# Seven block products for eight in the gate and up projections, and the down projection's weights kept in scratch memory

## The reference

```
x = layernorm(x + self_attention(x))
x = layernorm(x + cross_attention(x, ctx))
W[k,n] = scales[g_idx[k],n] * (w4[k,n] - (z4[g_idx[k],n] + 1))     # for gate, up, down
h   = silu(x @ Wg) * (x @ Wu)       # [1792,1024] @ [1024,2752], twice
out = layernorm(x + h @ Wd)         # [1792,2752] @ [2752,1024]
```

## Time and profile before

| what | value |
|---|---|
| median of 3 runs | 1928.49 us (1924.17 to 1934.58) |
| profiled execution | 1928.87 us, span 1927.2 us |
| PE busy | 1816.8 us, 94% of the span |
| DVE busy | 855.8 us, 44% |
| ACT busy | 445.2 us, 23% |
| POOL busy | 393.0 us, 20% |
| matmuls of 128x448, f16, in gate, up and elsewhere | 4464, busy 863.4 us |

### The profile page before, as it was taken

How to read it: one execution, slowest core, us unless ns; L and a number is a source line. 1 busy time by engine, 2 the same in 40 slices (tenths; PEclk the granted TensorE clock), 3 DMA queues, 4 the chain that set the end, 5 groups by cost and what they waited for, 6 DMA issues and landing times.

```text
span 1927.2 us, 26598 instructions
## 1 busy us (share of the span) xinstructions
PE 1816.8 (94%) x10192; PEld 1023.6 (53%) x10192; DVE 855.8 (44%) x1333; ACT 445.2 (23%) x676; POOL 393.0 (20%) x277
## 2 busy tenths in 40 slices
PE   5798899897999869999999999999999999999998
PEld 3566644586878734454444445444545444444443
DVE  5688551656788854434443444344343210111111
ACT  3222110444565532222222222222221200000000
POOL 0222377233333321111111111111111100000000
PEclk9899999999999989999999999999999999999999
DMA  9242561699999942122112111211221321221220
GB/s 312 69 147 81 152 197 44 136 200 230 240 235 237 232 97 57 39 45 50 44 35 60 35 44 35 60 41 38 48 44 41 111 90 64 102 102 61 92 102 22
DMA packets 298812, 196.10 MB, mean 102 GB/s; under 512 B 258368, under 2 KB 272768, under 8 KB 296580
## 3 DMA queue, kind: packets, MB, share of 16 engines
q1 hardware_dynamic: 292516, 192.19, 39.4%
q10 hardware_dynamic: 6240, 3.15, 0.6%
HBM read 105.11 MB, written 50.34 MB: 81 GB/s over the span
## 4 chain that ended last, share of the span: by engine, by line
PE 54%; issue 26%; DVE 6%; DMA 6%; SPq 5%; POOL 2%; ACT 1%; POOLq 0%; DVEq 0%; ACTq 0%
PE psum L1306 52%; SPq L1738 4%; DMA arena<-arena 3%; DMA arena<-in_x 1%; DVE arena L725 1%; POOL small L944 1%; PE psum L1517 1%; POOL arena L953 1%; PE psum L1535 1%; DMA x_parts_scratch<-arena 1%; DMA arena<-in_L_xattn_Wq 1%; DVE arena L832 1%; DVE arena L500 1%; DVE logits L686 0%; DVE arena L406 0%
## 5 line engine op out<-in xcount | busy, mean ns | idle before, releaser
L1306 PE MATMUL psum<-arena 128*128 128x448 f16 (+7 forms) x9404 | 1746.9, 347 | 51.8 <-DMA arena<-arena 25.7
L1306 PEld LDWEIGHTS psum<-arena 128*128 128x128 f16 (+3 forms) x9404 | 973.1, 107 | 806.6 <-issue 92.5
L1060 POOL TENSOR_TENSOR arena<-arena 128x1024 f16<-128x1024 f32 (+1 forms) x64 | 136.1, 2126 | 659.0 <-ACT arena L1248 659.0
L886 DVE SCALAR_TENSOR_TENSOR arena<-psum,small,arena 128x448 f32<-128x448 f32 x84 | 57.4, 684 | 412.4 <-PE psum L1306 412.4
L926 DVE SCALAR_TENSOR_TENSOR arena<-psum,small,arena 128x512 f32<-128x512 f32 x28 | 21.0, 751 | 327.4 <-PE psum L1306 327.4
L944 POOL TENSOR_TENSOR small<-small 112x1 f32<-112x1 f32 (+1 forms) x46 | 49.9, 1084 | 507.3 <-DVE small L387 507.3
L1248 ACT ACTIVATE arena<-arena 128x1024 f16<-128x1024 f32 (+1 forms) x65 | 68.7, 1057 | 274.2 <-DVE arena L872 274.2
L1261 ACT ACTIVATE arena<-arena 128x448 f16<-128x448 f32 (+1 forms) x88 | 50.7, 577 | 289.0 <-DVE arena L886 289.0
L1018 POOL TENSOR_TENSOR arena<-arena 128x224 f16<-128x224 f32 x64 | 55.7, 870 | 126.2 <-ACT arena L1161 126.1
L870 DVE TENSOR_TENSOR arena<-arena,psum 128x1024 f32<-128x1024 uint32 x65 | 79.4, 1221 | 2.6
L892 DVE TENSOR_TENSOR arena<-arena 128x448 f16<-128x448 f32 (+1 forms) x88 | 55.0, 625 | 57.1 <-ACT arena L1261 57.1
(11 more groups left out here) (189 smaller groups left out, 756.2 us busy)
## 6 DMA issues: line engine op xcount, KB each, us to landing
h_scratch<-arena SPq DMA_DIRECT2D x84, 224.0 KB, 2.7
arena<-h_scratch SPq DMA_DIRECT2D x13, 1376.0 KB, 6.0
arena<-in_ctx SPq DMA_DIRECT2D x32, 512.0 KB, 5.4
arena<-in_x SPq DMA_DIRECT2D x32, 448.0 KB, 5.6
x_scratch<-arena SPq DMA_DIRECT2D x32, 448.0 KB, 3.6
arena<-in_L_ffn_down_qweight SPq DMA_DIRECT2D x21, 512.0 KB
x_parts_scratch<-arena SPq DMA_DIRECT2D x16, 448.0 KB, 5.5
arena<-in_ctx SPq DMA_DIRECT2D x16, 448.0 KB
```

The lines of the kernel that those rows point to most:

```text
L886: dve.scalar_tensor_tensor(h_f[0:n, :], up[0:n, :], sc_u[0:n, :], g_act[0:n, :], ALU.mult, ALU.mult).then_inc(s_hf, 1)
L1060: pool.tensor_tensor(dst[1], src, dst[0], ALU.subtract).then_inc(s_wl, 1)
L1306: mm = pe.matmul(out, a, r, start=(k == 0), stop=(k == len(pairs) - 1))
```

## The change

From chunk 4 to chunk 20 (17 chunks) gate and up are computed together with Strassen's scheme. The 1792 rows are cut in two halves and the inner dimension of 1024 in two halves; the two columns of the block product are gate and up. Eight block products of 12 matmuls (4 inner blocks by 3 passes) become seven, once for each `b` of two (448 rows of each half). The seven use four row operands that are sums (T1 to T4, made once, kept in `xsum`) and four weight operands that are sums (S1, S2, S3, S4, made for each chunk by `weight_sums`: four DVE operations of 512), besides plain blocks. Seven DVE additions of 448 and one ACT copy for each `b` put the results together (`six`, `quarters_second`, `gate_first`, `up_first`, `first_copied`).

The row sums are made during chunks 0 to 3, which keep the old products. A *pair* p is batch p and batch p + 8. For each of the 8 pairs SP loads both from `x2_d` into `xab` (`load_pair`), POOL makes the sums in place (`row_sums`), ACT writes two high parts (`sum_hi`), DVE two low parts (`sum_lo`), and SP transposes both into `xsum` (`load_sums`). There is one buffer `xab`: the next pair is loaded once both low parts of the last are made. Two pairs are handled in each of the chunks 0 to 3. In every list below, `chunk` is the function of an unchanged chunk (0 to 3, and 21).

```
+            def row_sums(p):            # POOL
...
+                pool.wait_ge(s_tx, TX0 + 32 * (p + 1))
+                pool.tensor_tensor(two2, two2, two1, ALU.subtract).then_inc(s_tb, 1)
+                pool.tensor_tensor(two1, two1, one1, ALU.subtract).then_inc(s_tb, 1)
+                pool.wait_ge(s_tb, TB0 + 4 * p + 2)
+                pool.tensor_tensor(one1, two2, one1, ALU.add).then_inc(s_tb, 1)
+                pool.wait_ge(s_tb, TB0 + 4 * p + 3)
+                pool.tensor_tensor(one2, one2, one1, ALU.subtract).then_inc(s_tb, 1)
...
             def chunk(i, s, more):
                 if more:
-                    for m in range(1 if known(i, NI) and i == NI - 2 else 2):
-                        low_part(3 * i + 2 + m, [wgu[1 - s][m][:, l, :, :] for l in range(2)], m)
+                    low_part(3 * i + 2, 1 - s, 0)
+                    row_sums(2 * i)
+                    low_part(3 * i + 3, 1 - s, 1, mixed(i + 1))
+                    row_sums(2 * i + 1)
...
+            def sum_hi(p, i):
+                act.wait_ge(s_tb, TB0 + 4 * p + 4 - 2 * i)
+                if p:
+                    act.wait_ge(s_tt[i], TT0 + 16 * p)
+                act.activation(xabp[i][0:S, 0, :].rearrange("p (c q) -> p c q", c=KC),
+                               xab[i][0:S, :].rearrange("p (q c) -> p c q", c=KC), ACT.Identity,
+                               scale=XF).then_inc(s_th, 1)
...
             def chunk(i, s, e, more):
+                q = 3 * i + 2
                 hidden(i, 0)
                 if more:
-                    dequant(3 * i + 2, 0, 1 - s, e + s)
+                    dequant(q, 0, 1 - s, e + s)
+                    sum_lo(2 * i, 1)
                 hidden(i, 1)
-                if more and not (known(i, NI) and i == NI - 2):
-                    dequant(3 * i + 3, 1, 1 - s, e + s)
+                if more:
+                    masked(q + 1, 1, 1 - s, e + s)
+                    scaled(q + 1, 1, s_cmb if mixed(i + 1) else None)
+                    if mixed(i + 1):
+                        weight_sums(q + 1, i + 1)
+                    sum_lo(2 * i, 0)
                 if is_last(i):
                     dequant(down_no(i), 2, s, i)
                 hidden(i, 2)
                 if not is_last(i):
                     dequant(down_no(i), 2, s, i)
+                    sum_lo(2 * i + 1, 1)
                 hidden(i, 3)
+                if not is_last(i):
+                    sum_lo(2 * i + 1, 0)
...
+            def load_pair(p):
+                if p:
+                    sp.wait_ge(s_tl, TL0 + 2 * p)
+                for i in range(2):
+                    sp.dma_start(xab[i][0:S, :], rows(x2_d, p + i * NB // 2)).then_inc(s_tx, 16)
+            def load_sums(p, i):
+                sp.wait_ge(s_tl, TL0 + 2 * p + 2 - i)
+                sp.dma_start_transpose(xsum[i].rearrange("p l k t -> p (l k) t")[:, :, p * S:(p + 1) * S],
+                                       xabp[i][0:S, :, :].rearrange("p l d -> p (l d)")).then_inc(s_tt[i], 16)
```

SP in `chunk`:

```
+                parts = NGATHER - 1 if is_last(i) else 3 * i + 2
+                sp.wait_ge(s_wf, parts)
+                sp.wait_ge(s_wh, parts)
+                sp.wait_ge(s_wl, parts)
+                if 1 <= i < NI - 1:
+                    store_wd(i - 1, 1 - s)
                 load_down(i, w_down)
                 if w_next:
                     load_chunk(i + 2, s, w_next)
-                if isinstance(i, int) and i == NI - 1:
+                if i < NP:
+                    load_pair(2 * i)
+                    for k in (1, 0):
+                        load_sums(2 * i, k)
+                    load_pair(2 * i + 1)
+                if is_last(i):
+                    sp.wait_ge(s_pr, PR0 + 14 * (NI - 1 - NP))
                     load_first_tile()
+                    for k in range(2):
+                        sp.wait_ge(s_wds[k], WS0 + 16 * (NI // 2 - 1))
+                    for k in range(3):
+                        load_wd(k)
                 for u in range(2):
                     sp.wait_ge(s_hh, 4 * i + 2 * u + 3)
                     sp.wait_ge(s_hl, 4 * i + 2 * u + 3)
-                    half = slice(u * TT // 2, (u + 1) * TT // 2)
-                    for l in range(2):
...
+                if i < NP:
+                    for k in (1, 0):
+                        load_sums(2 * i + 1, k)
```

PE in the 17 changed chunks, and its wait ahead of them:

```
+            def mixed_chunk(i, s, e):
+                last = known(i, NI)
+                for b in range(2):
+                    v = 2 * (i - NP) + b
+                    bank = mixed_banks(s, b)
+                    if b == 0:
+                        pe.wait_ge(s_wl, 3 * i)
+                    pe.wait_ge(s_ad, AD0 + 7 * v - 5)
+                    seventh(bank[0], s, "G1", "X11", b)
+                    if b == 0:
+                        if last:
+                            gather_last(3 * i + 2, 1 - s, e + s)
+                        else:
+                            gather_gu(3 * i + 2, 0, 1 - s, e + s)
+                        pe.wait_ge(s_wl, 3 * i + 1)
+                    pe.wait_ge(s_ad, AD0 + 7 * v - 2)
+                    seventh(bank[1], s, "S2", "T2", b)
+                    if b == 1:
+                        gather_down(down_no(i), i)
+                    pe.wait_ge(s_ad, AD0 + 7 * v - 1)
+                    seventh(bank[2], s, "S1", "T1", b)
+                    pe.wait_ge(s_ad, AD0 + 7 * v)
+                    seventh(bank[3], s, "S3", "T3", b)
+                    if b == 0 and not last:
+                        gather_gu(3 * i + 3, 1, 1 - s, e + s)
+                    pe.wait_ge(s_cp, CP0 + v + 1)
+                    seventh(bank[0], s, "S4", "X22", b)
+                    pe.wait_ge(s_ad, AD0 + 7 * v + 1)
+                    seventh(bank[1], s, "G2", "X21", b)
+                    pe.wait_ge(s_ad, AD0 + 7 * v + 4)
+                    seventh(bank[2], s, "U2", "T4", b)
...
+            with pe.Fori(NP // 2, NI // 2 - 1) as e:
                 for s in range(2):
-                    chunk(2 * e + s, s, e, True)
-            chunk(NI - 2, 0, NI // 2 - 1, True)
+                    mixed_chunk(2 * e + s, s, e)
+            mixed_chunk(NI - 2, 0, NI // 2 - 1)
```

DVE there:

```
+            def mixed_chunk(i, s, e):
+                q = 3 * i + 2
+                last = known(i, NI)
+                v = 2 * (i - NP)
+                bank = mixed_banks(s, 0)
+                dequant(q, 0, 1 - s, e + s)
+                six(v, 0, bank)
+                if not last:
+                    masked(q + 1, 1, 1 - s, e + s)
+                quarters_second(v, 0, bank)
+                if not last:
+                    scaled(q + 1, 1, s_cmb)
+                gate_first(v, 0, bank)
+                summed(v, 4)
+                hidden_f32(i, 0, g_d, g_c)
+                up_first(v, 0, bank)
+                hidden_lo(i, 0)
+                summed(v, 7)
+                hidden_f32(i, 1, g_b, g_a[0])
+                if not last:
+                    weight_sums(q + 1, i + 1)
+                hidden_lo(i, 1)
+                v, bank = v + 1, mixed_banks(s, 1)
+                six(v, 1, bank)
+                dequant(down_no(i), 2, s, i)
+                quarters_second(v, 1, bank)
+                gate_first(v, 1, bank)
+                summed(v, 4)
+                hidden_f32(i, 2, g_d, g_c)
+                hidden_lo(i, 2)
+                up_first(v, 1, bank)
+                summed(v, 7)
+                hidden_f32(i, 3, g_b, g_a[1])
```

More of the change, by code:

```diff
@@ L1263, in chunk, with high_sums @@
+            def high_sums(q, s):
+                act.wait_ge(s_wf, q + 1)
+                high_of_operands(s, 4, OPS)
+                high_of_operands(s, 2, 4).then_inc(s_wh, 1)
             def chunk(i, s, more):
+                q = 3 * i + 2
                 hidden(i, 0)
                 if more:
-                    high_part(3 * i + 2, wgu[1 - s][0][:, 0, :, :], 0)
+                    high_part(q, 1 - s, 0)
+                    sum_hi(2 * i, 1)
                 hidden(i, 1)
-                if more and not (known(i, NI) and i == NI - 2):
-                    high_part(3 * i + 3, wgu[1 - s][1][:, 0, :, :], 1)
+                if more:
+                    if mixed(i + 1):
+                        high_sums(q + 1, 1 - s)
+                    else:
+                        high_part(q + 1, 1 - s, 1)
+                    sum_hi(2 * i, 0)
@@ L1277, in _ @@
             for m in range(2):
-                high_part(m, wgu[0][m][:, 0, :, :], m)
+                high_part(m, 0, m)
             x2_hi(NB - 1, 1)
-            with act.Fori(0, NI // 2 - 1) as e:
+            for i in range(NP):
+                chunk(i, i % 2, True)
+            with act.Fori(NP // 2, NI // 2 - 1) as e:
                 for s in range(2):
-                    chunk(2 * e + s, s, True)
-            chunk(NI - 2, 0, True)
+                    mixed_chunk(2 * e + s, s, e)
+            mixed_chunk(NI - 2, 0, NI // 2 - 1)
@@ new lines, in seventh, with mixed_chunk @@
+            def seventh(out, s, weights, rows_, b):
```

(17 more changed lines are left out.)

394 lines of the change are left out of this document (291 added, 103 removed).

## The result

The changed kernel takes 1960.39 us (median of 4 runs, 1958.92 to 1965.4) against 1928.2 (1924.17 to 1934.58): ratio 1.0172, 95% interval 1.0148 to 1.0196. It is slower by a little under 2%, and inside the range, 15 us above the forecast. Its profiled execution spans 1958.2 us, 31.0 more than before.

The account below looks back on a forecast made before the run. Gate and up were taken to be bound by PE. From 1928.9 us, 65 lost in chunks 0 to 3, 63 saved in the 17 chunks and 14 lost at the end gave 1945 us, range 1898 to 1985.

Parts of the forecast that it names:

- The 17 chunks: Chunks 4 to 20, seven products for eight: 34.1 us per chunk for 37.84, 63 us saved, bounds 78 and 41.
- The wait at the gather of down: Chunks 4 to 20: PE's gather of down waits for DVE's last weight sum, 0.55 us in each chunk.
- my walk: One seven-product chunk stepped through from PE's first product at 0: last weight sum ends at 22.0, PE reaches down's gather at 21.45.
- the six more ends: Chunks 4 to 20: 14 shorter products for 8 add six product ends, 0 to 0.9 us per chunk, taken as 0.3.
- The upper bound of 35.4: Chunks 4 to 20: longest time per chunk in us, with the wait twice as long and ends at 0.15.
- Chunks 0 to 3: Row pairs form a serial chain that PE waits for: 48.7 us per chunk, loss 65 us in all, bounds 51 and 95.
- The stride: Chunks 0 to 3, reads at 32 bytes: sum_hi 2.09 us, sum_lo taken as 1.7, range 1.22 to 2.1.
- The end: End of gate and up: PE begins tile 0 at about +36 us after chunk 20, not +23; cost 14, upper bound 20.
- the small store's place in the queue: End of gate and up: the store of chunk 21's h stands behind 8.7 MB of loads, delaying PE's start; cost 13 us.
- My other case: End of gate and up: the queue lets the small store pass, PE starts at +23 and waits for groups; cost 6 us.
- B: Rival, chunks 0 to 3: the pairs hide and only the last transpose, about 5 us, is seen; 1885 us, chance 0.17.
- C: Rival, chunks 4 to 20: DVE, held by POOL, becomes the bound; 36.2 us per chunk, 1981 us in all, chance 0.18.

Follow-up runs that it names:

- The short low part: In chunks 0 to 3 POOL's low part of the down weights cut to 8 of 1024 columns, against the changed kernel: chunks 0 to 3 take 234.4 us for 240.8.
- the kernel with the small piece last: Changed kernel with all loads issued before the small second piece of tile 0's h, awaited by PE just before its use: end stretch 60.6 us for 67.6.
- the last pair early: Against one pair a chunk plus small piece last: pairs loaded and summed earlier, the last behind chunk 7's gate weights; 1886.57 us against 1929.82, ratio 0.9793.

## Why the prediction came out as it did

**The 17 chunks: right, 10 us too cautious.** 34.1 forecast, 33.42 measured. The wait at the gather of down came where I had put it and for the reason given, but with 0.13 us for 0.55. In the trace, from PE's first product of a chunk on, DVE starts the addition behind the seventh product at 16.96 (17.05 in my walk), PE would reach the gather at 21.40 (21.45), and the last weight sum ends at 21.47 (22.0). I had added full durations on DVE (0.69 for each sum), but the starts of these sums lie 0.60 to 0.72 apart. Without the wait PE needs 33.29, and not 33.55: the six more ends, for which I took 0.3 us, cost 0.04. The upper bound of 35.4 should be 35.25 by its own terms. DVE's last weight sum and PE are within 0.1 us of each other here; by this reading a longer chain on DVE at that place would cost at once, which no run shows. The stretch gained 72.6 and not 17 x 4.42 = 75, since chunk 4 began at a lower clock.

**Chunks 0 to 3: right mechanism, mis-sized by 23 us.** The engines that wait, and the places, are those named. In chunk 0 the chain held to its steps up to the second transpose: the pair at 733.4 (735 forecast), the first `sum_lo` 7.0 behind it (6.9), up weights 12.5 (12.65), the second `sum_lo` 17.6 (17.55). Then three terms were short, for 5.9 of the 6.0 us that a chunk took longer:
- From there to the second pair's landing: 8.0 us for 6.6. I counted one load at 0.35; the pair is two, and their issue takes 1.72.
- The third `sum_lo` ended 9.1 behind its pair's landing, not 6.9: it took 4.44. I had POOL's fourth sum ahead of it, not POOL's low part of the down weights, which follows without a gap. The short low part shows that it is this, 1.4 us a round by itself in the mean of three.
- From the last `sum_lo` to the next landing: 14.9 for 12.55, in the second transpose and SP's chunk head.

In chunk 3 the pairs lie 30.9 us apart, for 25.6 in the other chunks: there the weight sums and their high and low parts lie on the path, and I had counted the sums alone, 2.9. Three chunks were 18.5 us longer and chunk 3 was 6.1 longer; less the 1.6 at the start that is 23. The stride was within its bounds. `sum_lo` took 1.99 undisturbed; I took 1.7, and the end of 2.1 was right. The Trainium skill (SBUF — State Buffer, section Door 1: The DMA port swizzle) says that full rate needs two hits in a line of 16 bytes. The trace agrees, 1.99 us for 1.21 in order, and the 2.1 that I had worked out for that rule is nearer than my 1.7. Since POOL's last sum overlapped it, this cost little.

**The end: right sum, half the reason.** 16.4 for 14, and PE began at +36.8 for +36. As forecast, no wait for a group is on record. (My line of sum was loose: +6.6 and 22 to 25 us are +29 to +32, not +30 to +33, and 13 and 1.7 are nearer 15.) But I took the small store's place in the queue for the whole cost. With the place mended only 7.0 came back; the groups, which had been hidden behind that wait, take over as the bound at once. My other case, PE at +23 and waits for groups, cost 6 in my count; the kernel with the small piece last shows it, at 9.4.

**The sum.** 15 us of difference are 22.9 of loss too little in chunks 0 to 3, 9.6 too much loss in the 17 chunks and 2.4 too little at the end, less 0.8 in the other stretches. That two of them run against each other is luck: with the 17 chunks as forecast the total would have been 25 us above 1945.

**Rivals.** My range began at 1898 and so left out B's own time, 1885, though I wrote that it took in most of B. B, that the pairs hide, fell for this order of work, but one pair a chunk hides wholly: its argument by shares was sound for half the load. C fell twice, by the period and by the doubled low parts. By the Trainium skill (SBUF — State Buffer, SBUF: two separate sides) the shared port is held for a whole instruction. Single operations agree (4.44 for 2.35 us, 1049 for 680 ns); the period of chunks 4 to 20 did not get longer by it when POOL's work was nearly doubled. It cost time on the chain of chunks 0 to 3, and ahead of chunk 8 in the versions with one pair a chunk.

## What to carry to other kernels

A chain through four engines and two DMAs costs its latency wherever an in-order engine must meet it; spread it so thin that each meeting finds the data there, even if the saving then starts some rounds later (four chunks given up for 18 us won back 79 of the 88, and 84 with the last pair early). To cost such a chain, list what each engine starts in the midst of every step, too: that was the term that the walk left out. When a wait ends on a small transfer behind a large one, ask what the large one would cost if the small one were first: here more than half stayed.

## What the hardware showed beyond that

- SP itself stands while much is queued. The issue of one store of h takes 0.43 us in the median of the changed kernel and 5.3 behind the large loads (nanoseconds, then issue to landing in us):
```profile
L2217 SPq DMA_DIRECT2D h_scratch<-arena x88: 380/431/5345, 754.4 to 1554.8; - x88
...
DMA to landing us min/median/max: 2.4/2.9/18.4
```
- Behind each long wait PE ran at the lower of its two clocks for some us. After 22.6 us of standing, the first 12 matmuls of chunk 4 took 4.66 us for 2.3. In chunks 0 to 3 the same makes most of the 12 us that no wait explains.
- Code ahead of chunk 0 that was the same in all kernels took 706.0 to 717.3 us. What makes that is open.
